# Expert tiles numbered in three stages of counts, seven of them with half the rows, the first tiles interleaved with the last attention steps

## The chip, the cores and the metric

The kernel runs on one core of a Trainium2 chip. The metric is the device time in microseconds (us) of one execution. The engines are TensorE (PE; its weight loads are shown apart as PEld), VectorE (DVE), ScalarE (ACT), GpSimd (POOL) and SyncE (SP), whose queue issues most DMAs. Each engine works through its own instructions in order and waits on semaphores.

## What is computed

A cross-attention layer over 8 batches of 256 tokens with width 256 and 16 heads, and behind it a mixture of 8 experts of which every token uses the two with the largest gates. The biases and the output projection of attention are left out here.

```python
x = x + xattn(layernorm(x), ctx, ctx, Wq, Wk, Wv, Wo, bo, pad_mask, mask)
gate = softmax(layernorm(x) @ w_gate.T)            # (2048, 8)
topk_scores, topk_idx = top_k(gate, 2)
cw = (one_hot(topk_idx, 8) * topk_scores[..., None]).sum(axis=1)
h = gelu(einsum('td,edh->teh', flat_x, W1) + b1)   # 256 -> 1024
y = einsum('teh,ehd->ted', h, W2) + b2             # 1024 -> 256
x = x + einsum('ted,te->td', y, cw)
```

## The kernel before

**Attention in steps.** One attention step `s` is a pair of heads of one batch: step `8n + m` computes pair `m` of batch `n`. Steps run from -16 to 84. TensorE computes scores for the row maxima (L818, tile S1) in step `s`, VectorE takes their maximum (L512), and ten steps later (`LAG`) TensorE computes the scores again in the other orientation (L841, S2), ScalarE takes the exponential (L709) and TensorE multiplies with V (L853). So the last maximum is in step 63 and the last exponential in step 73. What a batch needs besides (projections, layer norms, output projection, gates, ranks, list positions) hangs on a table `due` that says in which step each engine does it; `FRONT`, `BACK`, `ROUTE` and their LATE forms hold the numbers. In a step an engine does what is due in the order of its code.

**K and Q** of a batch are written by DMAs into one of four buffers each (`HELD`), six batches of normalised rows `x2n` are kept (`KEPT`).

**Routing.** For the groups of batches (0,1), (2,3), (4,5), (6), (7) the kernel finds each token's two experts, counts tokens ahead of it (TensorE `count`, L885), and GpSimd writes the normalised row with its token number and gates to two places in a list in DRAM, by indirect DMAs (L431, 8 for a group of two batches, 4 for one). Every expert has a region there; the first 256 rows of each region and a spare piece are cleared beforehand.

**The seam.** When all attention is done, every engine waits for all of it (`attention_over`), since the expert buffers take the memory of the attention buffers. The weights of tiles 0 and 1 were loaded in steps 59 and 60.

**Experts in tiles.** 23 tiles of 256 list rows each: tile `i` < 8 is the first 256 rows of expert `i`; tiles 8 to 22 are chosen by a table that VectorE works out during the first tiles from all counts. For each tile TensorE turns the rows (L1100), computes the hidden layer in four pairs of 128 hidden units (L1116, 48 matmuls of 256 columns), and the output one tile later (L1129, 48 matmuls of 256 columns). Numbers are split into a high and a low part, so ScalarE rounds weights (L1154, L1163), rows and hidden values (L1189) and VectorE subtracts (L1290, L1297, L1330). ScalarE does the Gelu (L1181); VectorE adds the bias and scales (L1340, L1344); GpSimd adds the rows to the output by indirect DMA (L1223). SP loads rows (L1081) and both weights (L1047, L1050; 1 MB each). Ahead of tile 8 SP clears 256 rows behind each expert's last list row (L1073), waits for that, and only then loads tile 8.

## Time and profile before

| | before |
|---|---|
| median of 3 runs | 564.59 us (564.55 to 566.5) |
| the profiled execution's own time | 570.19 us |
| its span, first to last instruction | 569.0 us |
| PE, PEld busy | 487.9 us, 419.8 us |
| DVE, ACT, POOL busy | 375.3, 344.8, 174.1 us |
| granted TensorE clock, mean | 0.91 |

The profile shows one execution, which took 5.6 us more than the median. Lines name the kernel's source line (L1116), the engine and the operation, with out<-in tiles. TensorE's granted clock is a share of 2.4 GHz. Matmuls overlap, so the length of one says less than the length of a row of them.

### The profile page before, as it was taken

What the parts mean: (1) busy time and instruction counts of PE and PEld (TensorE: products, weight loads), DVE (VectorE), ACT (ScalarE), POOL (GpSimd) and SP (SyncE); (2) the same over time, 40 slices, a digit from 0 to 9 for tenths busy, and PEclk for the clock granted to TensorE, in tenths of its full rate; (3) what the DMA queues carried; (4) which work ended last, traced back from release to release, by engine and by line L of the source; (5) the groups of instructions that cost most, each with busy time, mean ns of one, the idle gap of its engine ahead of it and who ended that gap; (6) DMA issues with size and microseconds to landing.
All of it is one profiled execution on the core that took longest, in us unless ns stands there. A gap on an engine that the chain in (4) does not pass through costs nothing.

```text
span 569.0 us, 10658 instructions
## 1 busy us (share of the span) xinstructions
PE 487.9 (86%) x3925; PEld 419.8 (74%) x3925; DVE 375.3 (66%) x737; ACT 344.8 (61%) x567; POOL 174.1 (31%) x192
## 2 busy tenths in 40 slices
PE   5888899999988576441699999599999999999994
PEld 3455666667656353331699999599999999999994
DVE  4556668677777524056387888288887888878861
ACT  2025666676554333104388888288878888788870
POOL 4215023433214552306003432223223422234224
PEclk9998999999988767555599999799999999999998
DMA  6683533444108321103627879868878778677713
GB/s 209 205 246 144 201 122 145 146 141 150 60 22 293 118 78 47 49 18 95 217 94 212 253 237 252 238 212 260 241 200 238 234 249 253 200 231 239 218 20 37
DMA packets 73014, 97.10 MB, mean 171 GB/s; under 512 B 7168, under 2 KB 59776, under 8 KB 72960
## 3 DMA queue, kind: packets, MB, share of 16 engines
q1 hardware_dynamic: 62720, 84.53, 44.5%
q0 software_dynamic: 8160, 10.38, 9.5%
q10 hardware_dynamic: 2080, 1.49, 0.9%
q8 instruction: 33, 0.54, 0.4%
q14 instruction: 21, 0.17, 0.1%
HBM read 63.96 MB, written 17.34 MB: 143 GB/s over the span
## 4 chain that ended last, share of the span: by engine, by line
PE 69%; issue 9%; DVE 7%; POOL 4%; ACT 4%; DMA 3%; SPq 2%; ACTq 1%; another core or an unknown queue 0%; POOLq 0%; DVEq 0%
PE h_bank L1116 21%; PE y_bank L1129 20%; PE bank L778 5%; PE bank L786 5%; PE S L818 4%; PE bank L853 3%; DVE nmax L512 3%; PE S L841 2%; PE bank L770 2%; PE x_bank L1100 2%; POOL lists L431 2%; PE S L891 2%; DMA xg<-lists 1%; PE bank L861 1%; PE bank L870 1%
## 5 line engine op out<-in xcount | busy, mean ns | idle before, releaser
L1223 POOL DMA_INDIRECT out<-y,slot x46 | 83.8, 1821 | 212.8 <-DVE y L1344 178.1
L1116 PE MATMUL h_bank<-xgT,W1p 128*128 128x256 f32 x1104 | 144.4, 288 | 1.7 <-DVE xgT L1315 1.7
L1116 PEld LDWEIGHTS h_bank<-xgT,W1p 128*128 128x128 f32 x1104 | 138.2, 194 | 2.2 <-issue 2.2
L1129 PE MATMUL y_bank<-W2p,hp 128*128 128x256 f32 x1104 | 136.0, 282 | 0.0
L1129 PEld LDWEIGHTS y_bank<-W2p,hp 128*128 128x128 f32 x1104 | 133.9, 188 | 0.0
L512 DVE TENSOR_REDUCE nmax<-S 128x4 f32<-128x1024 f32 x64 | 78.4, 1224 | 52.9 <-PE S L818 48.0
L709 ACT ACTIVATE prob<-S 128x1024 f32<-128x1024 f32 x64 | 65.7, 1027 | 42.7 <-PE S L841 37.7
L1330 DVE TENSOR_TENSOR hp<-hf,hp 128x512 fp32r<-128x512 f32 x92 | 63.6, 691 | 35.9 <-ACT hp L1189 35.7
L1290 DVE TENSOR_TENSOR W1p<-w_in,W1p 128x1024 fp32r<-128x1024 f32 x46 | 56.2, 1226 | 21.1 <-ACT W1p L1154 21.0
L1181 ACT ACTIVATE hf<-h_bank,b1c 128x256 f32<-128x256 f32 x120 | 49.8, 466 | 28.4 <-PE h_bank L1116 28.4
L1297 DVE TENSOR_TENSOR W2p<-w_in,W2p 128x1024 fp32r<-128x1024 f32 x46 | 56.3, 1225 | 10.0 <-ACT W2p L1163 10.0
L1189 ACT ACTIVATE hp<-hf 128x512 fp32r<-128x512 f32 x92 | 58.2, 633 | 2.9
L408 POOL TENSOR_TENSOR rstd<-ve,half 128x2 f32<-128x2 f32 x16 | 11.4, 714 | 146.1 <-DVE ve L497 146.0
L1154 ACT ACTIVATE W1p<-w_in 128x1024 fp32r<-128x1024 f32 x46 | 47.9, 1044 | 13.6 <-DMA w_in<-in_W 8.8
L1163 ACT ACTIVATE W2p<-w_in 128x1024 fp32r<-128x1024 f32 x46 | 47.9, 1044 | 0.0
L431 POOL DMA_INDIRECT lists<-x2n,rows x32 | 32.3, 1008 | 31.7 <-DVE rows L614 23.2
L818 PEld LDWEIGHTS S<-K,Q 64*128 64x128 f32 x256 | 19.6, 189 | 26.4 <-issue 14.0
L853 PE MATMUL bank<-prob,V 128*32 128x256 f32 x512 | 37.8, 417 | 1.2 <-ACT prob L709 1.2
L818 PE MATMUL S<-K,Q 64*128 64x256 f32 x256 | 33.0, 337 | 6.3 <-DVE nmax L512 5.6
L1181 ACT ACTIVATE hf<-h_bank,b1T 128x256 f32<-128x256 f32 x64 | 26.6, 466 | 16.7 <-PE h_bank L1116 16.7
L841 PE MATMUL S<-Q,K 64*128 64x256 f32 x256 | 29.1, 308 | 2.5 <-ACT prob L709 1.2
L1100 PE MATMUL x_bank<-ident,xg 128*128 128x128 f32 x92 | 14.9, 287 | 18.0 <-DMA xg<-lists 18.0
(144 smaller groups left out, 535.4 us busy)
## 6 DMA issues: line engine op xcount, KB each, us to landing
w_in<-in_W SPq DMA_DIRECT2D x46, 1024.0 KB, 9.0
K<-flat_k SPq DMA_DIRECT2D x24, 256.0 KB, 2.4
Q<-flat_q SPq DMA_DIRECT2D x24, 256.0 KB
xg<-lists SPq DMA_DIRECT2D x23, 265.0 KB, 5.6
lists<-zero SPq DMA_DIRECT2D x17, 265.0 KB, 3.8
b_in<-in_b SPq DMA_DIRECT2D x23, 128.0 KB, 6.6
cin<-in_ctxT SPq DMA_DIRECT2D x8, 256.0 KB, 3.8
xin<-in_x SPq DMA_DIRECT2D x8, 256.0 KB, 4.1
```

Source lines behind the costliest of these rows:

```text
L512: max_done.after(dve.tensor_reduce(nmax[n % 4][:, :, :, m].rearrange("p t r -> p r t"), S1[:].rearrange("p r (t k) -> p r t k", t=TT), AX. ...
L709: exp_done.after(act.activation(prob[s % 4][:].rearrange("p r t l -> p (r t l)"), S2[:].rearrange("p r l -> p (r l)"), ACT.Exp, scale=SCALE))
L818: i = pe.matmul(S1[:, r, t * L:(t + 1) * L], Q[n % HELD][a, m, t * P:(t + 1) * P], K[n % HELD][a, m, :], start=not masked, stop=(not maske ...
L853: i = pe.matmul(b[j * OS:(j + 1) * OS, 0:L], V[n % 3][:, t, r * MP + m, :], prob[(MP * n + m) % 4][:, r, t, :], start=(t == 0), stop=(t == ...
L1116: ins = pe.matmul(h_bank[pair][:, u, :], W1p[k][a][:, kc, m * P:(m + 1) * P], xgT[k][c][:, kc, :], start=(j == 0), stop=(j == len(terms) - 1))
L1129: ins = pe.matmul(y_bank[k][:, t, :], hp[k][a][:, m, t * P:(t + 1) * P], W2p[k][c][:, m, :], start=(j == 0), stop=(j == len(terms) - 1))
L1181: h_act.after(act.activation(hf[pair % 2][:, u], h_bank[pair][:, u], ACT.Gelu, bias=bias[:, m:m + 1]))
L1189: h_hi.after(act.activation(hp[i % 2][0][:, c], hf[pair % 2][:], ACT.Copy))
L1223: st_y[i % 4].after(pool.indirect_dma_start(out=out, out_offset=bass.IndirectOffsetOnAxis(ap=slot[i % 4][:, t:t + 1], axis=0), in_=y[i % 2 ...
L1290: w1_lo.after(dve.tensor_tensor(W1p[i % 2][1][:, c], w1_in[i % 2][:, c], W1p[i % 2][0][:, c].bitcast(F32), ALU.subtract))
L1297: w2_lo.after(dve.tensor_tensor(W2p[i % 2][1][:, c], w2_in[i % 2][:, c], W2p[i % 2][0][:, c].bitcast(F32), ALU.subtract))
L1330: h_lo.after(dve.tensor_tensor(hp[i % 2][1][:, c], hf[pair % 2][:], hp[i % 2][0][:, c].bitcast(F32), ALU.subtract))
```

## The change

Everything is in one memory plan: expert buffers no longer wait for `attention_over`, which is gone. The high and low parts of the weights lie in the K and Q buffers, of which there are three each instead of four; the hidden sums lie in S1 and S2. `KEPT` is 5. The projection of K comes three steps later (`k=-8`), that of Q one step later (`q=-6`).

Groups are now (0,1), (2,3), (4), (5), (6), (7). After group 2 (step 68), group 4 (step 78) and group 5 (step 84) a matmul `total` gives the counts so far; from them VectorE makes the table in three stages. Stage 1 names 3 tiles of 256 rows out of lists that are that full already, stage 2 names 4 more, stage 3 names 9 tiles of 256 rows and 7 of 128 rows for what is left. So there are still 23 tiles, but 16 of them have 256 rows and 7 have 128, and from tile 8 on the kinds alternate: 7 and 8 whole, then whole and half in turn, ending with a half one. All tiles take their weights by a table entry.

A tile's four pairs are now `units`. Units 0 to 10 (tiles 0 and 1 and three pairs of tile 2) are done in steps 74 to 84, one in each step, at the end of what the engine does in the step; the rest follow in a loop. Output matmuls of the tile before stand between the pairs. There is one output bank instead of two. Clearing of the eight regions beforehand is gone; the clearing behind the last rows (now ahead of tile 7) stays.

```diff
+    EARLY, NEXT = 3, 4
+    WHOLE = TOP * NT * P // TS - EARLY - NEXT
+    PARTS = NE - 1
+    order = [(TS // P, c) for c in range(EARLY + NEXT)]
+    for j in range(WHOLE):
+        order.append((TS // P, EARLY + NEXT + j))
+        if j >= WHOLE - PARTS:
+            order.append((1, EARLY + NEXT + j + PARTS))
+    NTILE = len(order)
+    UNIT_STEP = 74
-    KEPT = 6
-    HELD = 4
+    KEPT = 5
+    HELD = 3
-    FRONT = dict(load=-16, ln1=-13, norm1=-11, residual=-10, k=-11, k_split=-10, k_stack=-10, xn=-8, xT=-7,
-                 q=-7, q_split=-6, q_stack=-6, mask_q=-3, v=-1, v_out=0, mrep=7, mx=8)
+    FRONT = dict(load=-16, ln1=-13, norm1=-11, residual=-10, k=-8, k_split=-7, k_stack=-7, xn=-8, xT=-7,
+                 q=-6, q_split=-5, q_stack=-5, mask_q=-3, v=-1, v_out=0, mrep=7, mx=8)
+    LISTED = {0: (2, 68), 1: (4, 78), 2: (5, 84)}
+        W1p = [[v[:].rearrange(flat_of).rearrange("p (k f) -> p k f", k=KC) for v in (Q[i], K[i])] for i in (2, 1)]
+        W2p = [[Q[0][:], K[0][:]], [w[:] for w in W2_1]]
+        h_bank = [S[:, r].rearrange("p (u l) -> p u l", u=2) for S in (S1, S2) for r in range(2)]
+        SP_TILES = {69: (0, 1), 76: (2,), 79: (3,)}
+        def sp_tile(i):
+            k, c = i % 2, column[i]
+            sp.wait_ge(table_done.sem, stage_of(i))
...
+            ld_xg[k].after(sp.dma_start(xg[k][:, 0:HT[i]], lists[bass.ds(first_row, HT[i] * P), :]
+                                        .rearrange("(t p) e -> p t e", p=P)))
...
+            if i >= 2:
+                sp.wait_ge(w1_lo.sem, 2 * (i - 1))
+            ld_w1[k].after(sp.dma_start(w1_in[k][:], w1))
+            if i >= 2:
+                sp.wait_ge(w2_lo.sem, 2 * (i - 1))
+            ld_w2[k].after(sp.dma_start(w2_in[k][:], w2))
+        POOL_TILE = 82
+                if "total" in now and now["total"] < 2:
+                    for _ in lists_of(now["total"]):
+                        pass
+                if s in (UNIT_STEP - 3, UNIT_STEP - 2):
+                    w1_low(0, s - UNIT_STEP + 3)
+                if s == UNIT_STEP - 1:
+                    rows_low(0)
+                if s >= UNIT_STEP:
+                    dve_unit(s - UNIT_STEP)
+        def hidden(i, pair):
+            k, q, n = i % 2, 4 * i + pair, HT[i] * P
...
+                for j, (kc, a, c) in enumerate(terms):
+                    ins = pe.matmul(h_bank[pair][:, u, 0:n], W1p[k][a][:, kc, m * P:(m + 1) * P], xgT[k][c][:, kc, 0:n],
+                                    start=(j == 0), stop=(j == len(terms) - 1))
+        def pe_unit(u):
+            i, pair = divmod(u, 4)
+            hidden(i, pair)
+            if pair == 1 and i + 1 < NTILE:
+                turn_tile(i + 1)
+            if i and 2 <= pair < 2 + HT[i - 1]:
+                outputs(i - 1, pair - 2)
+        def dve_experts():
+            working = lists_of(2)
+            for u in range(UNITS_IN_STEPS, 4 * NTILE):
+                for _ in range(8):
+                    next(working, None)
+                dve_unit(u)
-        A.close()
-        for engine in (sp, act, dve, pe, pool):
-            attention_over(engine)
```

The order of the instructions at three places. First ScalarE before, from its last exponential of attention (prob<-S) to the first tile's Gelu (hf<-h_bank); W1p<-w_in and W2p<-w_in round weights, lg<-lg is a group's gate exponential.

```order
L709 ACTIVATE prob<-S 128x1024
L668 ACTIVATE OT<-bank 128x256
L720 ACTIVATE lg<-lg 128x16
L668 ACTIVATE aT<-bank 128x512
L668 ACTIVATE yT<-bank 128x512
L720 ACTIVATE lg<-lg 128x16
L1154 ACTIVATE W1p<-w_in 128x1024 x2
L1163 ACTIVATE W2p<-w_in 128x1024 x2
L1154 ACTIVATE W1p<-w_in 128x1024 x2
L1197 ACT_TABLE_LOAD
L1197 ACTIVATE b1c<-b1T 128x1
```

The same engine in the changed kernel, from the exponential of step 71 on; weights are now rounded into Q (L1027).

```order
L1133 ACTIVATE prob<-S 128x1024
L1092 ACTIVATE OT<-bank 128x256
L1027 ACTIVATE Q<-w_in 128x1024
L1092 ACTIVATE yT<-bank 128x512
L1133 ACTIVATE prob<-S 128x1024
L1048 ACTIVATE xgT<-bank 128x512
L1092 ACTIVATE OT<-bank 128x256
L1058 ACT_TABLE_LOAD
L1058 ACTIVATE hf<-S,b1c 128x256 x2
L1071 ACTIVATE hp<-hf 128x512
L1027 ACTIVATE Q<-w_in 128x1024
L1144 ACT_TABLE_LOAD
```

The two roundings of W1 of tile 0 moved ahead of the exponentials of steps 72 and 73, and exponentials of gates now stand between Gelus, with a table load at each change: five loads behind the first instructions of the kernel where one stood.

Second SP before, from the last K and Q DMAs of attention: weights of tiles 0 and 1 (L338, L339) ahead of the last stores (L328), the rows of tile 0 (xg) behind.

```order
L338 DMA w_in<-in_W 128x2x1024
L339 DMA w_in<-in_W 128x8x256
L338 DMA w_in<-in_W 128x2x1024
L339 DMA w_in<-in_W 128x8x256
L328 DMA out<-x 128x2x256 x3
L1056 DMA b_in<-in_b 128x256 x2
L1081 DMA xg<-lists 128x2x265 x3
```

And SP in the changed kernel at the same place, where each tile first reads its table entry (TENSOR_LOAD table).

```order
L369 TENSOR_LOAD table
L369 ISA x2
L370 TENSOR_LOAD table
L370 ISA x2
L390 ISA
L390 DMA xg<-lists 128x2x265
L395 ISA
L395 DMA w_in<-in_W 128x2x1024
L398 DMA w_in<-in_W 128x8x256
L401 ISA
L401 DMA b_in<-in_b 128x256
```

No weight is loaded before the table of stage 1 is there.

Third GpSimd before, around the routing of groups 1 and 2 (lists<-x2n,rows are the indirect DMAs, rstd the layer norms of batches 6 and 7).

```order
L431 DMA lists<-x2n,rows 18688x265
L431 DMA lists<-x2n,rows 18688x265 x7
L431 DMA lists<-x2n,rows 18688x265
L431 DMA lists<-x2n,rows 18688x265 x7
L408 TENSOR_TENSOR rstd<-ve,half 128x2 x2
L431 DMA lists<-x2n,rows 18688x265
L431 DMA lists<-x2n,rows 18688x265 x3
```

And in the changed kernel.

```order
L567 DMA lists<-x2n,rows 18688x265
L567 DMA lists<-x2n,rows 18688x265 x7
L567 DMA lists<-x2n,rows 18688x265
L567 DMA lists<-x2n,rows 18688x265 x3
L546 TENSOR_TENSOR rstd<-ve,half 128x2
L567 DMA lists<-x2n,rows 18688x265
L567 DMA lists<-x2n,rows 18688x265 x3
L546 TENSOR_TENSOR rstd<-ve,half 128x2
```

Four of the sixteen DMAs that stood ahead of batch 6's layer norm now stand behind it.

## Rows read from the trace of the kernel before

**Rows 1.** The page: the span in 40 slices, PE, its granted clock, DMA.

```profile
PE   5888899999988576441699999599999999999994
PEclk9998999999988767555599999799999999999998
DMA  6683533444108321103627879868878778677713
```

**Rows 2.** Stretches: busy us (count) of PE, PEld, DVE, ACT, POOL; clock, DMA, GB/s.

```profile
212.00:236.90 24.90, 10.82 (x82) 6.80 (x82) 7.82 (x32) 8.38 (x11) 8.43 (x9) 0.67 0.16 54
236.90:263.40 26.50, 13.81 (x66) 10.04 (x66) 12.00 (x60) 2.01 (x5) 4.61 (x5) 0.50 0.09 32
263.40:276.70 13.30, 1.11 (x6) 0.89 (x6) 7.89 (x10) 7.87 (x9) 5.67 (x26) 0.50 0.40 108
276.70:359.70 83.00, 82.76 (x675) 82.59 (x676) 62.96 (x113) 66.24 (x118) 18.85 (x11) 0.97 0.72 221
381.00:535.00 154.00, 154.00 (x1298) 154.00 (x1296) 124.07 (x209) 127.23 (x222) 48.73 (x27) 1.00 0.77 234
```

**Rows 3.** The seam in order of time: start, us, engine, line, idle before.

```profile
235.79 1.02 ACT L709 ACTIVATE prob<-S 128x1024 f32<-128x1024 f32 x1
263.24 0.16 DVE L614 CAST rows<-ends 128x2 int32<-128x2 f32 x1
269.68 1.28 ACT L1197 ACT_TABLE_LOAD   x1
276.68 5.46 PE L1116 MATMUL h_bank<-xgT,W1p 128*128 128x256 f32 x24 [1.50 <-DVE xgT L1315]
300.78 3.10 PE L1116 MATMUL h_bank<-xgT,W1p 128*128 128x256 f32 x24
303.72 2.56 PE L1129 MATMUL y_bank<-W2p,hp 128*128 128x256 f32 x20
```

**Rows 4.** PE in order of time, runs of matmuls at full clock.

```profile
304.80 4.84 PE L1129 MATMUL y_bank<-W2p,hp 128*128 128x256 f32 x39
173.13 1.09 PE L861 MATMUL bank<-ident,OT 128*128 128x128 f32 x8
176.04 1.95 PE L870 MATMUL bank<-WgT,yT 128*128 128x8 f32 x16
103.28 1.99 PE L778 MATMUL bank<-xT,WqT 128*128 128x256 f32 x8 [0.64 <-ACT xT L668]
```

**Rows 5.** Waits between 172 and 240 us: total, times, longest.

```profile
DVE x2n L503 <- POOL rstd L408: 9.8, 1, 9.8
```

**Rows 6.** One tile on ScalarE in order of time, and two VectorE operations of routing.

```profile
402.57 0.84 ACT L1181 ACTIVATE hf<-h_bank,b1c 128x256 f32<-128x256 f32 x2 [1.93 <-PE h_bank L1116]
403.44 0.63 ACT L1189 ACTIVATE hp<-hf 128x512 fp32r<-128x512 f32 x1
403.98 1.04 ACT L1154 ACTIVATE W1p<-w_in 128x1024 fp32r<-128x1024 f32 x1
414.46 0.84 ACT L1181 ACTIVATE hf<-h_bank,b1c 128x256 f32<-128x256 f32 x2 [1.93 <-PE h_bank L1116]
244.23 0.17 DVE L565 RECIPROCAL sm<-sm 128x2 f32<-128x2 f32 x1
244.43 0.17 DVE L566 TENSOR_TENSOR lg<-lg,sm 128x16 f32<-128x16 f32 x1
```

**Rows 7.** The stall at tile 8 in order of time: SP's queue and PE.

```profile
349.35 9.67 SPq L1073 DMA_DIRECT2D lists<-zero  x8
362.39 0.41 SPq L1081 DMA_DIRECT2D xg<-lists  x1
365.81 1.11 PE L1100 MATMUL x_bank<-ident,xg 128*128 128x128 f32 x4 [5.82 <-DMA xg<-lists]
```

**Rows 8.** DMA issues on the page: count, KB each, us to landing.

```profile
w_in<-in_W SPq DMA_DIRECT2D x46, 1024.0 KB, 9.0
K<-flat_k SPq DMA_DIRECT2D x24, 256.0 KB, 2.4
```

More of the change, by code:

```diff
@@ L132, in build @@
             due[LATE_ROUTE[i][name] if i in LATE_ROUTE else MP * ns[-1] + o][name] = i
+    for stage, (i, step) in LISTED.items():
+        due[step]["total"] = stage
     top = ExitStack()
@@ L206, in build @@
-        larger = sb(A, "larger", [P, GMAX, NE, NE])
-        equal = sb(A, "equal", [P, GMAX, NE, NE])
-        rank = sb(A, "rank", [P, GMAX, NE])
-        off = sb(A, "off", [P, GMAX, NE])
-        more = sb(A, "more", [P, NE])
-        ends = sb(A, "ends", [P, 2, GMAX])
-        first = ExitStack()
-        masks_in = sb(first, "masks_in", [P, NB * L * L // P], U8)
-        line = sb(first, "line", [2 * D, L])
-        first.close()
-        prob = [sb(A, f"prob{i}", [P, 2, TT, L]) for i in range(4)]
+        S1 = top.enter_context(nc.psum_tensor("S1", [P, 2, TT * L], F32))
@@ new lines, in build @@
+        rank = sb(top, "rank", [P, GMAX, NE])
+        off = sb(top, "off", [P, GMAX, NE])
+        more = sb(top, "more", [P, NE])
+        ends = sb(top, "ends", [P, 2, GMAX])
+        with ExitStack() as first:
+            masks_in = sb(first, "masks_in", [P, NB * L * L // P], U8)
+            line = sb(first, "line", [2 * D, L])
+        with ExitStack() as overlaid:
+            prob = [sb(overlaid, f"prob{i}", [P, 2, TT, L]) for i in range(4)]
+            flat = {w: [sb(overlaid, f"flat_{w}{i}", [P, KC, L], F32R) for i in range(2)] for w in "qk"}
+            xin = [sb(overlaid, f"xin{i}", [P, TT, E]) for i in range(2)]
+            cin = [sb(overlaid, f"cin{i}", [P, KC, L]) for i in range(2)]
+            V = [sb(overlaid, f"V{i}", [P, TT, H, 2 * D]) for i in range(3)]
+            OT = [sb(overlaid, f"OT{q}", [P, L]) for q in range(NQ)]
+            WqT, WkT, WvT = (sb(overlaid, f"W{w}T", [P, KC, E]) for w in "qkv")
+            xn = sb(overlaid, "xn", [P, TT, E])
@@ new lines, in build @@
+        scale = [sb(top, f"scale{i}", [P, TS // P]) for i in range(4)]
+        table = sb(top, "table", [P, 2, NTILE], I32)
+        zrow = sb(top, "zrow", [P, NE], I32)
+        number = sb(top, "number", [P, WHOLE])
+        bounds = sb(top, "bounds", [P, CHUNKS])
+        index = sb(top, "index", [P, NE])
+        origin = sb(top, "origin", [P, NE])
+        taken = sb(top, "taken", [P, NE])
+        cnt = sb(top, "cnt", [P, NE])
+        full = sb(top, "full", [P, NE])
+        passed = sb(top, "passed", [P, NE, CHUNKS])
@@ L287, in sp_attention, with sp_experts @@
+        def sp_experts():
+            for i in range(sum(len(t) for t in SP_TILES.values()), NTILE):
+                sp_tile(i)
+            for k in range(4):
+                sp.wait_ge(st_y[k].sem, scatters(max(i for i in range(NTILE) if i % 4 == k)))
         def sp_attention():
@@ L434, in scatter @@
                                 in_=x2n[:, n % KEPT, t], in_offset=None))
+            pool_r.after(pool.memset(taken[:], 0.0))
+            for k in range(CHUNKS):
+                pool_r.after(pool.memset(bounds[:, k:k + 1], float(TS * (k + 1))))
+            for k in range(WHOLE):
+                pool_r.after(pool.memset(number[:, k:k + 1], float(k)))
             for s in range(START, LAST):
@@ L664, in act_attention, with act_unit, act_experts @@
+        def act_unit(u):
+            i, pair = divmod(u, 4)
+            gelu(i, pair)
+            hidden_high(i, pair)
+            if pair < 2 and i + 1 < NTILE:
+                w1_high(i + 1, pair)
+            if pair >= 2:
+                w2_high(i, pair - 2)
+            if pair == 1 and i + 1 < NTILE:
+                rows_high(i + 1)
+        def act_experts():
+            for u in range(UNITS_IN_STEPS, 4 * NTILE):
+                act_unit(u)
         def act_attention():
```

890 lines of the change are left out of this document (450 added, 440 removed).

## Prediction

> **What bounds the kernel now.** I read the slices first: PE is 90% busy or more in the second half and half idle between slices 14 and 18, where its granted clock is down to 0.5 [rows 1]. Then the stretches [rows 2]. From 381 to 535 us PE is busy all 154.00 us at clock 1.00, DVE 124, ACT 127 and the DMA engines 77%, so the expert stage is bound by TensorE. One tile lasts from one wait of ACT for its first hidden pair to the next, 402.57 to 414.46: 11.89 us, for 48 hidden, 48 output and 4 turning matmuls; ACT waits 1.93 us in it, so it works some 9.95 [rows 6]. Before that lies a stretch that no engine bounds: from the last exponential (235.79) over the last list position (263.24) to the first hidden matmul (276.68) PE is busy 13.81 of 26.5 and 1.11 of 13.3 us [rows 2, 3]. It is a chain of short operations of one batch that go from engine to engine. Three places are the change's: this seam, the tile's price, and the stall at tile 8.
>
> **Half tiles.** The page has matmuls of 256 columns in the tiles; a half tile has 48 hidden ones of 128 columns, 24 output ones of 256, and 2 turns. What a matmul costs comes from runs of them, first length taken off: 39 output matmuls last 4.84 us, with one's 0.28 off that is 4.56/38 = 0.120 us each. Does the price halve with the columns? Two rows say no: 8 turning matmuls of 128 columns last 1.09 us, (1.09-0.28)/7 = 0.116 each, and 16 matmuls of only 8 columns last 1.95 us, (1.95-0.26)/15 = 0.113 each, with the same 128 by 128 load ahead of each [rows 4] (0.28 and 0.26 are means of one). PEld is busy exactly as long as PE, 154.00 of 154.00 [rows 2]: the load sets a floor. Bounds for a half hidden matmul are 0.060 (half of 0.120) and 0.120; I take 0.113, since the 8-column row shows the floor. Even if such operands ran at the rate of the plain ones, 8 of 256 columns in 1.99 us, (1.99-0.39)/7 = 0.229, 128 columns would cost 0.114. So a half tile costs 48x0.113 + 24x0.120 + 2x0.116 = 8.5 us, and seven save 7x(11.9-8.5) = **-23.8 us**. By the Trainium skill, TensorE: Matmul & The Clock Gate, section LDWEIGHTS (loading the stationary operand), a load costs its columns over 1.2 GHz, 107 ns for 128, whatever the rows; by that a half hidden matmul costs 0.107 and the sum falls by 7x48x0.006 = 2 us. The trace's 0.113 agrees within overheads, and I keep it.
>
> Are the other engines in time? Weights are rounded in full for a half tile. A whole tile takes ACT 9.95 us; a half one keeps the four weight operations (next starts some 0.96 apart, from 1.04 less overlap) and has Gelus and roundings of half width: by the rows 0.84 for two Gelus and 0.63 for a rounding against 1.04 for twice its elements I estimate 7.9. A pair of tiles takes ACT 17.9, DVE (124.07/154.00x11.9 = 9.6, half 8) 17.6, PE 20.4; DMA is busy 0.77x11.9x2 = 18.3 less some rows. All fit, barely. Within a whole tile behind a half one PE needs only 8.9 us and ACT 9.95, made good in the next; I charge **+2** (0 to 14; it all goes to nothing if the pair lasts as before).
>
> **The seam.** The first 28.5 us of PE's expert work (276.68 to about 305.2, where hidden work of tiles 0, 1 and three pairs of tile 2 and three output halves are done [rows 3]; the second output half of three of 24 begins at 303.72) now lie in steps 74 to 84. I work out when step 84 ends.
> Up to the last exponential of attention, now 235.79: batch 6's layer norm waited 9.8 us for GpSimd [rows 5], which was in its indirect DMAs; four of these are now behind it and four earlier: -9.8. Ahead of the rank of group 3 VectorE now makes the table of stage 1, 22 operations at 0.21 from start to start (244.23 to 244.43 is 0.20 [rows 6]): +4.6, and TensorE waits for that rank. SP then loads rows and W1 of tile 0, which were long there: 1 MB lands in 9.0 us among others [rows 8], alone in perhaps 5; about 3 of it are not hidden, since ACT and DVE have W1's rounding in front of the exponentials of steps 72 and 73. One group more and the roundings themselves: +1.5. Together -0.8: last exponential at 235.
> Steps 74 to 84 take 26.4 us for attention alone (236.8 to 263.2). Bounds: not under PE's own work, 28.5 + 13.8 at half clock, some 8 at full, so 37; not over everything in series, 26.4 + 28.5 + four more table loads at 1.28 [rows 3] + table of stage 2 at 4.6 = 64.6. Each step ends in a unit whose next needs ACT and DVE, and each of the ten links of the last batch waits behind a unit on three engines, so it is nearer to the series: I take 52. Step 84 ends at 287, where before it was 305.2: **-18** (-33 to -5). Scatters of 4 or 5 us on GpSimd and the first add to the output in step 82 stand in line there, covered by the 16 units until tile 7.
> The three-buffer K and Q: K is due on SP 7 steps before use, Q 5 steps. Each batch's 8 steps last some 20 us, so 12 us and more for landings of 2.4 [rows 8]: 0. Uncovered it would cost what exceeds 12 us, in five batches.
>
> **Table of stage 3 and the stall.** Stage 3 has about 55 chained DVE operations instead of 17, eight turns of them in a unit: 38x0.2 = 7.6 us more in seven units, in which DVE has 20% free, some 4: **+3** (0 to 8). The clearing stall stays: 8 writes issued over 9.67 us, the rows of tile 8 at 362.39, and TensorE waits 5.82 us [rows 7]; tile 7's has the same distance and the same waits: 0 (up to -6 if the seam's slack lands there).
> **The end.** The last tile has one half to add: -2.
>
> **Sum.** -23.8 + 2 - 18 + 3 - 2 = -38.8. The profiled execution took 570.19 us (span 569.0), 5.6 above the median; against it the changed one should take 531, and against the median of 564.59 **526 us**.
>
> **Rivals.**
> *Tight seam.* PE's units fill the holes and steps 74 to 84 take 38 us: -32 for the seam, 512. For it speaks PE's 50% idle there; against it that every step has a link of attention ahead of the unit, and that DMA waits of 0.09 busy before turn into 4 MB of weights.
> *No floor.* Half hidden matmuls cost 0.060: 7x48x0.053 = 18 us less, 508. Against it is the 8-column row [rows 4]. The Trainium skill's page TensorE: Matmul & The Clock Gate, section Back-to-back issue gap, gives about 81 ns a matmul in a stream of loads and matmuls of 128 columns; by that the half tiles save 11 us more, 515. No row here shows 81.
> *Half tiles save nothing.* ACT, DVE and the weights' 2 MB are still due for each; if alternation makes them late, the pair lasts 23.8 and only the seam pays: 549. For it: 9.95 and 9.6 of 11.9, W1 landing 9.0 after issue with one tile's time. Decides if the issue of W1 to its rounding exceeds a short tile's 8.9.
> *Half clock in the seam.* Granted 0.67 and 0.50 in the tail of attention [rows 2]. If the units' short bursts keep it there, their 28.5 us become 57 and the seam takes 79: 553. The Trainium skill's page TensorE: Matmul & The Clock Gate, section HAM oscillation — how this bites in real kernels, says that bursts of matmuls between waits fall back to the lower clock each time; here the trace agrees for the tail without units. Against it: 0.97 as soon as dense work starts at 276.70.
> *Slower.* K and Q with three buffers are late: they can be written only when the scores of the batch three before are done, five to seven steps ahead of use. If a Q took 20 us from there instead of under 12, each of batches 3 to 7 waits 8 us, 40 in all, which eats the gain: 566, and slower beyond that. Landings of 2.4 us and a DMA share of a third to a half there speak against it [rows 1, 8].
> *Nothing happens*: the order moves, but the last chain of attention is as long as both halves in series: 64.6, 539; it lies within my range.
>
> **Chances.** Forecast 0.50 (its own range 514 to 539), tight seam 0.13, no floor 0.06, half tiles save nothing 0.11, half clock 0.11, slower 0.06, near no change 0.03. To leave out 2 in 10 at most the range goes from 507 to 552: it holds the forecast, both fast rivals, half tiles without gain and most of half clock. Under 0.5% (2.8 us) a measurement of this kernel can't tell from no change. Faster: 0.91; same 0.03; slower 0.06.
>
> **What would show it.** In the changed profile: runs of 128-column hidden matmuls at 0.11 to 0.12 us each (0.06 is no floor); a whole and a half tile together 20 to 21 us with PE busy throughout (23.8 with waits of ACT for w_in: third rival); the last exponential at 230 to 240 us; 48 to 56 us from there to the end of step 84, with clock above 0.8 (0.5: fourth rival); five table loads of 1.28 on ACT; a stall of some 6 us at tile 7; no wait of PE for K or Q in attention, whose steps up to 60 take what they took (173 us). Wrong it would be most likely in the 52 us of the seam, which I read from no row but put between two bounds.

## The result, and the profile after

The changed kernel takes 557.45 us (median of 4 runs, 556.83 to 559.61) against 564.57 for the kernel before in the same session (563.16 to 566.5): a ratio of 0.9856, 95% interval 0.9814 to 0.9898. It is faster, as forecast, and the interval lies wholly under 1, but by 7 us (1.4%) and not by 39, and the time lies outside the range of 507 to 552.

The profiled execution took 559.61 us, with a span of 558.2 against 569.0 before, so the traces differ by 10.8 us, 3.7 more than the medians (the profiled executions took 2.2 and 5.6 us more than theirs). I cut both at six marks: starts of exponentials (the first, the 50th, the last) and the moments at which TensorE turns the rows of tiles 4 and 8.

| stretch | before | after | difference | forecast |
|---|---|---|---|---|
| start to first exponential | 45.4 | 49.2 | +3.8 | 0 |
| first to 50th exponential | 127.8 | 140.1 | +12.3 | 0 |
| 50th to last exponential | 62.5 | 56.8 | -5.7 | -0.8 |
| last exponential to turn of tile 4 | 76.5 | 76.1 | -0.5 | -18 with the line above |
| turn of tile 4 to turn of tile 8 | 53.5 | 56.3 | +2.8 | +3 |
| turn of tile 8 to the end | 203.2 | 179.7 | -23.5 | -23.8 + 2 - 2 |

The last two lines came out as the forecast has them, though partly by luck (see below), and the two with the largest misses are attention's steady part and the seam. One execution says little about a difference of 3 us: in a second profile of the changed kernel (experiment 6) the first exponential starts at 46.1, the second to fourth stretches take 140.1, 54.5 and 73.0 us, and the last two 57.1 and 179.5. The changed kernel's time by stretches (us; busy time of each engine with its instructions; granted clock, DMA share, GB/s), which answers to [rows 2]:

```profile
49.20:189.30 140.10, 119.15 (x1095) 82.50 (x1096) 91.07 (x167) 82.81 (x124) 35.22 (x37) 1.00 0.28 96
246.20:306.50 60.30, 41.72 (x284) 39.21 (x284) 39.52 (x125) 37.51 (x59) 12.75 (x12) 0.83 0.50 168
306.50:322.20 15.70, 9.17 (x60) 9.08 (x61) 7.20 (x28) 3.59 (x7) 2.19 (x3) 0.78 0.22 68
322.20:378.50 56.30, 50.06 (x402) 49.69 (x401) 42.02 (x97) 39.91 (x69) 17.31 (x8) 0.94 0.78 231
378.50:528.00 149.50, 149.48 (x1270) 149.26 (x1269) 122.53 (x218) 126.97 (x239) 42.49 (x23) 1.00 0.84 250
```

The first line is a stretch in which TensorE is idle for 21 of 140 us at full clock. The second is the seam, up to the end of the third output half: the clock is 0.83, where [rows 2] had 0.67 and 0.50. The third, just behind it, has 60 matmuls in 15.70 us; in the kernel before the same 60 (62 records) took 7.10, from 305.2 to 312.3. From tile 8 on TensorE is busy 149.48 of 149.50 us.

**The seam and the hole.** The marks of the seam in order of time (start, us, engine, line, operation, idle before):

```profile
246.18 1.02 ACT L1133 ACTIVATE prob<-S 128x1024 f32<-128x1024 f32 x1 [0.27 <-PE S L1331]
301.86 0.18 PE L1385 MATMUL bank<-run,onesb 128*128 128x8 bf16 x1 [0.99 <-DVE run L946]
303.42 3.04 PE L1223 MATMUL bank<-W2p,hp 128*128 128x256 f32 x24
310.08 0.50 PE L1208 MATMUL S<-xgT,Q 128*128 128x256 f32 x2 [3.62 <-issue]
313.54 0.37 PE L1208 MATMUL S<-xgT,K 128*128 128x256 f32 x1 [2.95 <-issue]
314.13 0.41 PE L1208 MATMUL S<-xgT,K 128*128 128x256 f32 x1
315.87 0.84 ACT L1058 ACTIVATE hf<-S,b1c 128x256 f32<-128x256 f32 x2 [9.79 <-PE S L1208]
322.24 0.60 PE L1190 MATMUL bank<-ident,xg 128*128 128x128 f32 x4
```

Step 84, with unit 10 in it, ends 60.3 us behind the last exponential; I had put it at 52. Then TensorE stands for 3.62 us, runs two matmuls, stands for 2.95, and its next matmuls last 0.41 where they last 0.28 at full clock: of the 8.6 us that the stretch takes more than before, 6.57 are idle and some 2 are the clock's; ScalarE waits 9.79 us for its hidden pair. "issue" says that the profile shows nothing that TensorE waited for. At this place of its program the branch ends: it leaves the form without masks, jumps over the form with masks, and goes on with the experts. The profile counts the fetches of instructions too, queue q8 with 0.02 MB each. In the 14 us from 304 there are

```profile
q8 instruction: 3, 0.05, 1.4%
```

three of them, one in each of the microseconds that begin at 307, 311 and 315. The kernel before has the same jump, with one fetch in the microsecond at 262 and one at 267. TensorE stands there in any case, until the rows of tile 0 have landed:

```profile
274.10 1.08 PE L1100 MATMUL x_bank<-ident,xg 128*128 128x128 f32 x4 [12.15 <-DMA xg<-lists]
```

So the jump was paid there too, under a wait that was longer. The Trainium skill, Runtime: NRT & Kernel Launch, section Instruction fetch mechanics, says that a taken branch whose target lies outside the two pages at hand has to fetch the target page before execution goes on; the trace agrees.

**A step of attention.** The K of batch 5 (counted from 0) is projected here (the same columns), between two exponentials that start 4.97 us apart:

```profile
108.89 1.02 ACT L1133 ACTIVATE prob<-S 128x1024 f32<-128x1024 f32 x1 [0.77 <-PE S L1331]
109.25 0.66 PE L1260 MATMUL bank<-ident,xn 128*128 128x128 f32 x4
110.08 0.60 ACT L1092 ACTIVATE V<-bank 128x512 f32<-128x512 f32 x1
110.83 1.97 PE L1268 MATMUL bank<-cin,WkT 128*128 128x256 f32 x8 [0.92 <-ACT V L1092]
113.06 0.40 PE L1331 MATMUL S<-Q,K 64*128 64x256 f32 x4
113.86 1.03 ACT L1133 ACTIVATE prob<-S 128x1024 f32<-128x1024 f32 x1
```

TensorE turns xn into one of the two shared banks, wants the other for K, finds V in it, waits 0.92 us until ScalarE has emptied it, and only after K's 1.97 us come the scores for the next exponential. Before, K stood three steps earlier, in a step without these neighbours. All that TensorE waits for between 49.2 and 189.3 us (total, times, longest) is

```profile
PE S L1308 <- DVE nmax L855: 15.9, 17, 1.6
PE bank L1268 <- ACT V L1092: 4.6, 5, 0.9
```

the maxima that the scores' bank waits for, and this bank five times; no K and no Q is late.

### The profile page after: what moved, and what is told of

It reads as the page before. It is cut to its first block, busy times and chain, and to the rows that moved or that the text cites. A ratio compares the mean times of both kernels' runs of the same rounds, so it can differ in the third digit from the quotient of the medians.

```text
span 558.2 us, 10523 instructions
## 1 busy us (share of the span) xinstructions
PE 464.9 (83%) x3741; PEld 396.9 (71%) x3741; DVE 375.0 (67%) x837; ACT 336.3 (60%) x571; POOL 163.9 (29%) x197
## 4 chain that ended last, share of the span: by engine, by line
PE 49%; issue 17%; DVE 12%; ACT 8%; POOL 5%; DMA 5%; SPq 3%; ACTq 1%; another core or an unknown queue 0%; DVEq 0%; POOLq 0%
PE S L1208 14%; PE bank L1223 13%; PE bank L1268 6%; PE bank L1276 5%; DVE nmax L855 5%; PE S L1308 4%; DMA w_in<-in_W 3%; POOL lists L567 3%; ACT hf L1058 2%; PE S L1381 2%; PE bank L1343 2%; ACT W2p L1039 1%; ACT Q L1027 1%; PE S L1331 1%; PE bank L1260 1%
## 5 line engine op out<-in xcount | busy, mean ns | idle before, releaser
L1208 PE MATMUL S<-xgT,Q 128*128 128x256 f32 (+1 forms) x736 | 140.9, 292 | 3.6 <-issue 3.6
L1208 PEld LDWEIGHTS S<-xgT,Q 128*128 128x128 f32 x736 | 119.6, 201 | 7.0 <-issue 6.9
L1208 PE MATMUL S<-xgT,K 128*128 128x256 f32 (+1 forms) x368 | 106.4, 289 | 2.9 <-issue 2.9
L1058 ACT ACTIVATE hf<-S,b1c 128x256 f32<-128x256 f32 (+1 forms) x184 | 70.3, 433 | 52.0 <-PE S L1208 50.0
L758 DVE TENSOR_TENSOR hp<-hf,hp 128x512 fp32r<-128x512 f32 (+1 forms) x92 | 55.7, 606 | 35.4 <-ACT hp L1071 35.1
L1208 PEld LDWEIGHTS S<-xgT,K 128*128 128x128 f32 x368 | 73.9, 201 | 0.0
L725 DVE TENSOR_TENSOR K<-w_in,Q 128x1024 fp32r<-128x1024 f32 x46 | 56.3, 1224 | 22.5 <-ACT Q L1027 22.5
L1223 PE MATMUL bank<-W2p,hp 128*128 128x256 f32 x528 | 68.9, 287 | 1.5 <-DVE y L768 1.4
L1223 PEld LDWEIGHTS bank<-W2p,hp 128*128 128x128 f32 x528 | 66.0, 195 | 2.0 <-issue 1.7
L1027 ACT ACTIVATE Q<-w_in 128x1024 fp32r<-128x1024 f32 x46 | 48.2, 1048 | 14.8 <-DMA w_in<-in_W 14.6
L1071 ACT ACTIVATE hp<-hf 128x512 fp32r<-128x512 f32 (+1 forms) x92 | 52.1, 567 | 2.9
L567 POOL DMA_INDIRECT lists<-x2n,rows x32 | 32.2, 1006 | 20.7 <-DVE rows L960 12.4
```

Of the source, the lines that this page charges most:

```text
L567: st_list[n % KEPT].after(pool.indirect_dma_start(out=lists, out_offset=bass.IndirectOffsetOnAxis(ap=rows[i % 2][:, k, u * TT + t:u * TT + ...
L725: w1_lo.after(dve.tensor_tensor(W1p[i % 2][1][:, c], w1_in[i % 2][:, c], W1p[i % 2][0][:, c].bitcast(F32), ALU.subtract))
L758: h_lo.after(dve.tensor_tensor(hp[i % 2][1][:, c, 0:n], hf[pair % 2][:, :, 0:n], hp[i % 2][0][:, c, 0:n].bitcast(F32), ALU.subtract))
L1027: w1_hi.after(act.activation(W1p[i % 2][0][:, c], w1_in[i % 2][:, c], ACT.Copy))
L1058: h_act.after(act.activation(hf[pair % 2][:, u, 0:n], h_bank[pair][:, u, 0:n], ACT.Gelu, bias=b1c[i % 3][:, 2 * pair + u:2 * pair + u + 1]))
L1071: h_hi.after(act.activation(hp[i % 2][0][:, 2 * pair:2 * pair + 2, 0:n], hf[pair % 2][:, :, 0:n], ACT.Copy))
```

## The experiments

My theory after the result had three parts: PLACES (the new steps of the K and Q projections on TensorE cost 12 to 16 us; the rival was BUFFERS, three in place of four), JUMP (the exposed jump costs 8 to 12; the rival was the table of stage 3), and half tiles worth what was forecast.

**1. K and Q in their old steps, in the changed kernel.**

```diff
-    FRONT = dict(..., k=-8, k_split=-7, k_stack=-7, ..., q=-6, q_split=-5, q_stack=-5, ...)
+    FRONT = dict(..., k=-11, k_split=-10, k_stack=-7, ..., q=-7, q_split=-6, q_stack=-6, ...)
```

> The changed kernel with the projections of K and Q and their splits back in the steps that they had before (K: 8n-11, split 8n-10; Q: 8n-7, split 8n-6); only the DMAs that write K stay at 8n-7, where the third buffer is free. Theory PLACES (the attention steps 10 to 59 are 12.2 us longer since K's projection now stands in the same step as the turning of xn and behind V's evacuation, so that one step per batch is crowded and others are empty): that stretch falls from 140 back to 128-130 us, the kernel from 557.5 to 541-546. Rival BUFFERS (three buffers make the DMAs late, or five kept batches do): the stretch stays at 138-141 and the kernel within 2 us of 557.5.

539.21 us, ratio 0.958 (0.9536 to 0.9625), 2 us under the range of PLACES, and from the first to the 50th exponential 128.2 us, with three buffers, where the kernel before has 127.8 with four. The buffers cost next to nothing, the steps do.

**2. The kernel before with the new steps** (the same line of FRONT, with four buffers).

> The kernel before, with four buffers and six kept batches, and only the row FRONT of the changed kernel (K's projection at 8n-8, its split and stack at 8n-7; Q's at 8n-6 and 8n-5). PLACES: the last exponential comes 12 to 16 us later than 235.8 us and the kernel takes 576-581. BUFFERS: no change, 563-566.

578.25 us, ratio 1.0302 (1.0258 to 1.0346), and 140.4 us from the first to the 50th exponential, where the changed kernel has 140.1: PLACES, shown from the other side.

**3. K alone and Q alone back**, each in the kernel of experiment 4 (ratio 0.9706).

> The changed kernel with TensorE's expert code in each branch, and only K's projection back in its old steps (from 8n-8 to 8n-11), Q's left where the change put it. The times between exponentials in the changed kernel's trace show two steps of each batch that are longer than before (4.97 us for 2.14, and 3.60 for 1.83). In the first TensorE turns xn, then waits 0.92 us for ScalarE to empty the bank that held V, then runs K's 8 matmuls of 1.97 us ahead of the next scores. Theory BANK: K's place, which puts three users of the two shared banks in adjoining steps, is the cost: this alone gives 10 to 13 us of the 13 to 16, 532 to 536 against 545 with both in the new places. Rival EACH: both share it, K 5 to 8 and Q the rest: 537 to 540.

> The same, with only Q's projection back in its old steps (from 8n-6 to 8n-7), K's left where the change put it. Theory BANK: Q's place is worth 0 to 3 us, 542 to 546. Rival EACH: 6 to 9 us, 536 to 540. A third way, ADJOINING: with Q one step behind K's and xn's step, three matmul groups follow each other and it is slower than with both in their new places, over 547.

K back: 534.58 us, ratio 0.9511 (0.9465 to 0.9556). Q back: 539.81, ratio 0.9579 (0.9549 to 0.9609). The times from one exponential of a batch to the next show where (batch 3, from each kernel's trace):

| kernel | 0 | 1 | 2 | 3 | 4 | 5 | 6 | 7 | sum |
|---|---|---|---|---|---|---|---|---|---|
| before | 2.26 | 2.59 | 2.69 | 2.59 | 2.26 | 3.34 | 2.14 | 2.89 | 20.8 |
| changed | 4.04 | 2.60 | 2.70 | 1.90 | 2.70 | 3.34 | 4.97 | 1.72 | 24.0 |
| K back | 4.04 | 2.59 | 2.69 | 2.59 | 2.25 | 3.34 | 2.14 | 1.74 | 21.4 |
| Q back | 2.26 | 2.59 | 2.69 | 1.91 | 2.71 | 3.34 | 4.97 | 2.87 | 23.3 |

K's place owns interval 6 (+2.83) and gains a little in 3; Q's owns interval 0 (+1.78) and wins back 1.17 in 7. By these K costs 2.6 a batch and Q 0.7, so BANK holds for K; Q's 539.8 us lies in the range of EACH, since the timed runs give it 4 to 10 us (0.9706 - 0.9579, with both intervals) where the 50 steps of its trace give 3.2. K by the same reckoning has 11 us where its trace gives 8.7. Experiment 4 ran on another chip than these two, so I go by the traces for the sizes. ADJOINING is refuted.

**4. The experts' code in each branch.**

```diff
         with nc.tensor.If(no_mask):
             pe_attention(range(LAST), masked=False)
+            pe_experts()
         with nc.tensor.Else():
             pe_attention(range(LAST), masked=True)
-        pe_experts()
+            pe_experts()
```

> The changed kernel with TensorE's remaining units (11 and on) written inside both branches of the mask test, instead of once behind them; nothing else moves. Theory JUMP (the idle 6.6 us of TensorE behind unit 10, put down to issue, and half the clock after it, are the jump from the end of the first branch over the other one, where instructions are not at hand): the stall between tile 3's turning and tile 4's (22.1 us for 11.9) goes, the kernel takes 546-550. Rival TABLE (VectorE's stage-3 table and the waits of unit 11 are late): the stall stays, 556-559.

545.07 us, ratio 0.9706 (0.9668 to 0.9744). One q8 fetch stands between 286 and 302.5, and TensorE has no idle time there by "issue". The turn of tile 4 comes 7.0 us behind the end of step 84 and unit 10, not 15.8, and 64.0 us behind the last exponential, not 76.1. The other 3.3 us of that are no part of the jump: step 84 ends 57.0 us behind the last exponential here and in the second profile of the changed kernel too, against 60.3 in the first. JUMP is shown; experiments 12 and 13 have it once more on one chip.

**5. No branch at all** (the masked form is left out of the program).

> The changed kernel without the mask test's branches: only the attention without mask is there (the inputs' masks are all true), so TensorE's instructions stand in one line. This leaves out the masked form. JUMP: as e4, 545-550, the stall between turnings 3 and 4 gone; if also the jump into the branch at step 0 costs something, up to 2 us less than e4. TABLE: 556-559.

544.16 us, ratio 0.9675 (0.9592 to 0.9759): the same as 4, within an interval of 5 us either way. So a branch costs nothing that can be told where its end does not stand in the way of the experts. Whether the price hangs on how much code is jumped over, no run shows.

**6. The changed kernel once more, as a control.**

> The changed kernel itself, as a control beside the others. In its profile ScalarE stands idle for 3.77 and 4.74 us ahead of two evacuations OT whose matmuls had long ended, in steps 60 to 73, and the last exponential of attention starts at 246.2 us; the profile of the kernel with the experts inside the branch has no such gap and that exponential at 238.4. Theory ACCIDENT: the gaps belong to one execution and not to the kernel; a second profile has the last exponential at 238 to 240 us and no gap of 3 us or more there. Rival PLACE: the order of the code makes them; the exponential is at 246 again. The idle time of TensorE behind unit 10, 3.62 and 2.95 us, and the half clock behind it must come back under either. Time: 0.98 to 0.99 of the kernel before.

555.89 us, ratio 0.9861 (0.9798 to 0.9923). TensorE's two idle times were there again, 4.00 and 2.51 us. ScalarE's gaps were there too, 3.91 and 3.12 us at other instructions of the same steps, with the last exponential at 240.6. Neither ACCIDENT nor PLACE describes that; see the end.

**7. Both repairs** (1 and 4).

> The changed kernel with both repairs: K and Q in the steps in which the kernel before had them, and the experts' code of TensorE inside each branch. Alone they gave ratios of 0.958 and 0.9706 against the kernel before, where the changed kernel has 0.9856. Theory SUM: the two losses lie in different stretches (steps 10 to 59, and behind unit 10) and add up: 0.9856 - 0.028 - 0.015 = 0.943, some 529 to 533 us, the tile 4 turning 24 to 28 us before where it does in the changed kernel (322.2). Rival HIDDEN: what one gives back, another wait takes (GpSimd's indirect DMAs and the landing of tile 0's weights don't move with PE), so that it stays at 537 to 540.

536.7 us, ratio 0.9514 (0.9461 to 0.9566), short of the sum's 0.943. It has ScalarE's gaps (4.72 and 3.26 us), which 1 and 4 had not and the changed kernel had: the sum of 0.943 mixes chips with and without them. With them throughout, the changed kernel has 0.9856, K and Q back 0.9647 (experiment 12) and both repairs 0.9503 (experiment 13), so the places are worth 0.021 (12 us) and, with them back, the code's place 0.014 (8 us), about as much as the traces of experiments 1 and 4 give each of them alone (11.9 and 8.7 us). That speaks for SUM, though 536.7 us is nearer to the range that I had given HIDDEN.

**8. All tiles with 256 rows** (both repairs; seven tiles take rows twice).

```diff
-    HT = [h for h, _ in order]
+    HT = [TS // P for _ in order]
```

> Both repairs, all 23 tiles with 256 rows (the table keeps its pieces, so seven tiles take rows twice, and the output is not the reference's). It measures the seven half tiles, my term -23.8. Theory FLOOR: a half tile saves 3.0 to 3.4 us and the last one's end 1 to 2: slower than the kernel with both repairs by 21 to 26, 551 to 558. Rival WEIGHTS: a half tile waits for its weights or ScalarE and saves less than 2 us: slower by under 14, 537 to 546.

560.29 us against 536.7 on the same chip: 23.6 us, by the ratios 0.9919 and 0.9514 23 (19 to 26). FLOOR, as forecast. In the traces, from the turn of tile 8 to the end, it is 203.1 against 181.3 us of experiment 7. The hidden matmuls of a half tile, in order of time in the changed kernel:

```profile
434.90 0.28 PE L1208 MATMUL S<-xgT,K 128*128 128x128 f32 x1
435.01 0.39 PE L1208 MATMUL S<-xgT,Q 128*128 128x128 f32 x2
435.23 0.28 PE L1208 MATMUL S<-xgT,K 128*128 128x128 f32 x1
```

Three of them start in 0.33 us, 0.111 each, where three of 256 columns take 0.36: half the columns save 8%. The half tile gains by its 24 output matmuls that fall away, not by its narrower hidden ones.

**9. No expert unit in attention's steps** (both repairs; `UNIT_STEP` 74 to 85, the first add to the output from step 82 to 84).

> Both repairs, but no unit of the experts in the steps of attention: all units behind step 84, the three stages and the half tiles stay. It measures what the first three tiles within attention are worth, the term that I put at -18. Theory WORTH: the holes of the last steps take 12 to 18 us of expert work, so this is 12 to 18 us slower than the kernel with both repairs: 541 to 549. Rival COVERED: the units delay attention's own chain by as much as they fill in, and stage 1's table and the weights are ready anyway, so it is within 3 us of it: 527 to 535.

541.8 us, ratio 0.9572 (0.9532 to 0.9611): 5 us over the kernel with eleven units in the steps on the same chip, so neither WORTH (12 to 18) nor COVERED (3).

**10. The same with the experts' code behind the branch.**

> K and Q in the old places, no unit of the experts in the steps of attention, and TensorE's expert code behind the branch, as before: the jump over the other form of attention now falls into the idle time behind step 84 as in the kernel before, whose trace has the two fetches of instructions (of 0.02 MB, queue q8, in the slices that begin at 262 and 267 us) inside TensorE's idle time from 263.24 to 276.68. Theory COVERED: in the kernel with the code in the branch TensorE waits 2.81 us behind its last attention instruction (260.05 to 262.86), so of the 6.5 to 10 us of a jump 3 are covered, and the rest with half clock behind it is seen: 3 to 8 us slower than the same kernel with the code in the branch (541.8), 545 to 550; in the kernel before, with 13.3 us of idle time, it was covered in full. Rival FREE: the jump costs only where units stand in the steps: within 2 us of 541.8.

534.58 us, ratio 0.9483 (0.9459 to 0.9507). COVERED failed: it was not slower than 9. That it was 7 us faster belongs to the chip or the session, which has no gaps of ScalarE: experiments 14 and 15 have both kernels on one chip, 0.3 us apart. The first hidden matmul stands behind this wait,

```profile
251.86 0.19 PE L1385 MATMUL bank<-run,onesb 128*128 128x8 bf16 x1 [0.53 <-DVE run L946]
255.41 0.76 PE L1208 MATMUL S<-xgT,Q 128*128 128x256 f32 x2 [3.36 <-DVE xgT L748]
```

3.36 us for the turned rows, where 9 had 2.81: of the jump at most 0.55 us is left. I had taken a jump for 6.5 to 10 us of TensorE's time; from the end of attention to the next matmul there are only 3.36 us here, in which it and the wait run side by side.

**11. Six units in the steps instead of eleven.**

> Both repairs, six units of the experts in the steps of attention (from step 79) in place of eleven (from step 74) or none. Eleven gave 536.7, none 541.8. With eleven, the last batch's chain took 54.4 us from the last exponential to step 84, where alone it takes 28.3, for 28.5 us of expert work: nearly all in series, since each link (choice of experts 4.25, layer norm 5.07, tags 2.29 us of TensorE's idle time) still waits behind units on VectorE and ScalarE. Theory SERIES: the gain comes only from what fits into the few long waits of the last batch, most of it in the later steps, so six units give as much as eleven or more: 534 to 538. Rival PROPORTION: each unit in a step saves alike: 539 to 540.

539.13 us, ratio 0.9559 (0.9532 to 0.9587). The time lies in PROPORTION's range, but both ranges were reckoned from kernels of another chip. On this chip the kernel without units took 534.58 (experiment 10, with the code behind, a difference that experiments 14 and 15 put at 0.3 us): six units lose 4.5 us against none, which neither SERIES nor PROPORTION allows. The trace agrees: from the last exponential to the end it takes 312.0 us, with none 307.9, and the first hidden matmul waits 6.23 us for its rows. Why six lose where eleven gain is open.

**12 to 15. Units or none, code behind or in: four kernels on one chip**, since the same four had run on three chips in experiments 1, 7, 9 and 10.

> First of four kernels on one chip, all with K and Q in the old places: units of the first tiles in attention's steps or not, TensorE's expert code in each branch or behind it. This one: units in the steps, code behind the branch (the changed kernel with the old places). From the last exponential to the end it took 312.7 us. Theory EXPOSED: the jump is paid in full only here, so this is the slowest of the four, 3 to 6 us over the same without units (540 against 535). Rival NOISE: it equals it within 2 us.

> Units in the steps, code in each branch. Its first profile had ScalarE idle for 4.7 and 3.3 us ahead of an evacuation and an exponential in steps 60 to 73, as other kernels of that chip, and the time came out 5 us over the sum of its two repairs. Theory EXPOSED and SUM: without those gaps it takes 530 to 533 us, the fastest of the four, some 7 to 8 under the one with code behind the branch. Rival HIDDEN: 535 to 537 also without the gaps.

> No units in the steps, code in each branch: first time 541.8 us, from the last exponential to the end 308.8. Theory EXPOSED: the jump is covered where no unit stands in the steps (TensorE waits 2.81 us for the turned rows in any case), so this equals the one with the code behind the branch within 2 us, 534 to 537 on a chip without ScalarE's gaps, and is 3 to 5 over the one with units. Rival: the code in the branch costs something by itself, 541 again.

> No units in the steps, code behind the branch: 534.6 us before, from the last exponential to the end 307.9. Theory EXPOSED: 534 to 536, 4 to 6 under the one with units and the code behind the branch: as the changed kernel is built, its first three tiles within attention lose time against the same stages without them. Rival NOISE: the 534.6 was the chip, and it is at 538 to 541.

| | code behind the branch | code in each branch |
|---|---|---|
| eleven units in the steps | 546.07, 0.9647 (0.961 to 0.9683) | 539.79, 0.9503 (0.9468 to 0.9538) |
| no unit in the steps | 543.25, 0.9579 (0.9549 to 0.9609) | 542.95, 0.9568 (0.9526 to 0.961) |

EXPOSED holds in its signs: the code's place is worth 6.3 us with units in the steps (0.0144 of 567 is 8) and 0.3 without; the units are worth -3.2 us with the code in the branches and +2.8 with it behind, where it is in the changed kernel. The second sign is less sure, as the interval of the difference, 0.0068, is about 0.005 either way. The absolute times I had expected for a chip without ScalarE's gaps; this chip had them, and all four came out 6 to 10 us above.

## Why the prediction was wrong

**K and Q, put at 0: the step that failed first.** "K is due on SP 7 steps before use, Q 5 steps. [...] So 12 us and more for landings of 2.4: 0." That sum is right and concerns the wrong thing. I costed the transfer that a moved projection feeds, and not the projection: its 8 matmuls, 2 us in all, and the bank that they want, put into a step that turns xn just behind V. It costs 12.3 us between the first and the 50th exponential (experiments 1 to 3). By the timed runs it is 12 us where both kernels have ScalarE's gaps (0.9856 - 0.9647 of 565, experiment 12) and 16.3 in the kernel before (experiment 2); what the 4 us between them are is open. The rival "slower" had the place right and the mechanism wrong: no K and no Q landed late.

**The seam, -18.** Step 84 was forecast 52 us behind the last exponential and came at 60.3; the same work lay 69.4 us behind it before (235.79 to about 305.2 [rows 3]). So -9.1 (-12.4 in the second profile, where it is 57.0), for the 17.4 that 52 meant: I chose 52 too far from the series. But the sum also ended there. I never asked what had lain under the idle time that the units were to fill. The jump did: before, it was covered by 12.15 idle us; the change laid it bare, with half clock behind it, 15.7 us for work of 7.1, +8.6. The two leave -0.5.

**And the -18 was set against the wrong neighbour.** I compared units in the steps with the kernel before. Most of the gain needs no unit in attention: with none (experiment 10) the first hidden matmul starts 29.2 us behind the last exponential, before 40.9 (276.68 - 235.79). That is the staged table's and the one memory plan's; no run takes the two apart. The units then add only 3 to 5 us, and that with the code in the branches, since they run in series with attention: steps 74 to 84 take 25.9 us without them (experiment 10: 226.16 to 252.05) and 57.0 with all 28.5 us of units in them (experiment 4: 238.45 to 295.43), where the two in series would be 54.4. What they save is what the same work loses behind attention, waits of 3.36 and 3.90 us and the lower clock: it ends at 63.7 there. TensorE's idle time inside the seam of the changed kernel stays, by the waits between 246 and 303.4 us (total, times, longest):

```profile
PE bank L1375 <- DVE chosen L927: 8.9, 2, 4.7
PE bank L1260 <- DVE x2n L846: 5.1, 1, 5.1
PE bank L1260 <- DVE ao L879: 2.4, 1, 2.4
PE bank L1343 <- ACT prob L1133: 1.7, 1, 1.7
```

The holes were not filled: from the last exponential to the last list position TensorE waits 16.6 us in all with units (experiment 4) and 14.2 without (experiment 10). As I read it, each link of the last batch stands on VectorE and ScalarE behind the unit that was to fill its hole.

**Up to the last exponential, -0.8.** -5.7 behind the 50th exponential, of which I had named a cause (GpSimd's DMAs out of the layer norm's way): VectorE's wait for rstd, 9.8 us [rows 5], is 0.9 us in that stretch of the changed kernel. No run tests it by itself, and I set too much against it. +3.8 ahead of the first exponential I had not looked at, and one profile each does not size it: in the second profile of the same kernel the first exponential is at 46.1 (+0.7), and in its variants between 46.0 and 49.3. What sets it is open.

**Half tiles, -23.8 + 2, and the end, -2.** The half tiles are right: from the turn of one tile to that of the next the changed kernel takes 8.60 and 11.8 us in turn where before it took 11.89 each time, 3.3 us a half tile, so 23.1 for seven; 23.6 by removal. "I take 0.113, since the 8-column row shows the floor" was measured at 0.111. The +2 did not come, and the end got 2 us longer instead of shorter: with whole tiles TensorE takes 28.40 us from the turn of the last tile to its last matmul (experiment 8), before 26.42, and it stands twice for VectorE's y, 1.70 us, which it did not before. There is one output bank now instead of two; no run tests that. That the line of the table reads -23.5 all the same is luck: 2.3 us of it belong to the stall, as the next paragraph shows. The rivals *no floor* and *half tiles save nothing* are out: between 378 and 528 us the waits of ScalarE for its weights are

```profile
ACT Q L1027 <- DMA w_in<-in_W: 5.5, 6, 2.0
```

5.5 us in six times, and TensorE idles 0.02 us. The Trainium skill, TensorE: Matmul & The Clock Gate, section Back-to-back issue gap, has about 81 ns for a matmul in a stream of 128 columns; the runs here differ, 111, and decide.

**Stage 3 and the stall, +3.** The number, +2.8, is right and the reason mostly not. Two tiles of the changed kernel and one of the kernel before, each from its turn to the next (the columns of [rows 2]):

```profile
334.19:347.30 13.11, 12.17 (x103) 12.00 (x101) 12.34 (x24) 10.06 (x18) 7.21 (x2) 1.00 0.73 212
364.70:378.50 13.80, 13.80 (x100) 13.80 (x101) 8.01 (x13) 9.67 (x17) 0.00 (x0) 0.85 0.73 255
365.81:380.01 14.20, 14.20 (x101) 14.20 (x101) 8.89 (x15) 9.66 (x17) 0.00 (x0) 0.82 0.69 249
```

VectorE makes the table of stage 3 from 307.3 to 334.6, in part under TensorE's two stops at the jump. It is behind with its other work then, and in the next tile, the first line, TensorE waits once for its y, 0.94 us; the tile takes 1.2 us over the usual 11.9. That is what stage 3 costs here, for my +3 (without the jump the same wait is 1.68, experiment 4). The other two lines are the tile behind the stall, at a lower clock. The stall moved one tile ahead, so this tile lies between the turns of tiles 4 and 8 now (+1.9), and lay behind the turn of tile 8 before (2.3 of the -23.5). The stall's own tile took 17.40 us for 17.88.

**Half clock in the seam** did not happen (0.83), **tight seam** neither (60.3 for 38).

In the traces the forecast misses by 28 us (-10.8 for -38.8), by the medians by 32: in the traces 12 by K and Q, 9 by the jump, 8 by the seam proper (5 in the second profile), 4 by the start (1 in the second), less 5 that the tail of attention gave. The two costs that I had put at nothing are 21 of the 28, and both could have been read: a projection's 8 matmuls are in [rows 4], and the branch is in the code.

## What to carry to other kernels

When a step is moved, price the instructions where they land, with the banks their neighbours hold, before the transfers that they feed; intervals between one recurring instruction, listed by position in the loop, show the cost at once. When idle time is filled, list everything that used to lie under it: a jump over code, a table load, a fetch. Measure an interleaving against the same stages without it: here it was worth 3 to 5 us at best, lost 3 with the code behind the branch, and I had put it at 18. And set side by side only kernels that ran side by side: the same kernel had 0.958 and 0.9647.

Both repairs together gave the best kernel of those that ran side by side, 539.79 us against 566.97 for the kernel before (0.9503), and 0.9514 in another session. Without units in the steps and with the code behind the branch it was 543.25 (0.9579) in the first of these, 3.5 us more with intervals that do not meet; its 0.9483 is of a chip without ScalarE's gaps, on which both repairs together did not run.

## What the hardware showed that I had not expected

TensorE's jump over the skipped, unrolled form of attention shows as idle time by "issue", and as fetches on a queue of their own. It costs 3.6 to 4.0 us, a second stop of 2.5 to 3 two matmuls later, and half clock behind (the changed kernel twice, experiments 1 and 12); next to nothing, 0.3 us by experiments 14 and 15, when TensorE must wait anyway.

ScalarE stands idle for 2 to 6 us, ahead of an evacuation or exponential whose matmuls had long ended, between the 50th and the last exponential of ten profiled executions and in none of the other eight. In the second profile of the changed kernel:

```profile
205.33 1.02 ACT L1133 ACTIVATE prob<-S 128x1024 f32<-128x1024 f32 x1 [3.91 <-remote]
216.59 0.38 ACT L1092 ACTIVATE OT<-bank 128x256 f32<-128x256 f32 x1 [3.12 <-remote]
```

"remote" says that no releaser is in the trace. Kernels of one chip all had it or all had not (those of experiments 1 to 5, 10 and 11 had not). With it the changed kernel and its variants take 54.5 to 57.1 us from the 50th to the last exponential, without it 48.7 to 50.9. So part of the gap between kernels of different sessions is the chip's or the session's: the same kernels had 0.958 without it and 0.9647 with it (experiments 1 and 12), and 0.9483 and 0.9579 (10 and 15). The sum of the two repairs on a chip without it, 0.943, was not measured. What holds ScalarE there is open.
